# Third layer's experts: tokens sorted by expert into 29 tiles, in place of every expert over every token

## What is computed

```
def _L2_ffn_ref(h, router_w, w1, b1, w2, b2):
    B, S, D, E, F = (2, 256, 128, 14, 256)
    ...
    logits = x @ router_w
    assignments = jnp.argmax(logits, axis=-1)
    probs = jax.nn.softmax(logits, axis=-1)
    weights = jnp.take_along_axis(probs, assignments[:, None], axis=1)[:, 0]
    hid = jnp.einsum('nd,edf->nef', x, w1) + b1
    hid = jax.nn.gelu(hid, approximate=False)
    all_out = jnp.einsum('nef,efd->ned', hid, w2) + b2
    sel = jnp.take_along_axis(all_out, assignments[:, None, None], axis=1)[:, 0, :]
    moe_out = (sel * weights[:, None]).reshape(Bb, Ss, Dd)
...
x = x + jnp.tanh(g_ffn[2]) * _L2_ffn_ref(_layernorm(x, axis=-1), ...)
```

## Time and profile before

| | us |
|---|---|
| median of 3 runs | 1395.78 (1394.82 to 1402.14) |
| the profiled execution | 1410.47 |
| its span | 1408.4 |
| PE busy | 1127.7 (80%) |
| DVE, ACT, POOL busy | 910.1, 788.3, 554.4 |
| granted TensorE clock, mean | 0.882 of full |
| third layer's routing and experts, first and last instruction | 810.94 to 1010.5 |

### The profile page before, as it was taken

The page is one execution under the profiler, slowest core; times in us unless marked ns, Lnnn a source line. Parts: engine busy times, 40 slices in busy tenths (PEclk is TensorE's granted clock), DMA queues, the critical chain, the costliest instruction groups (busy, mean ns, idle before and its releaser), DMA issues. The chain is left out here.

```text
span 1408.4 us, 30563 instructions
## 1 busy us (share of the span) xinstructions
PE 1127.7 (80%) x10377; PEld 540.0 (38%) x10377; DVE 910.1 (65%) x1742; ACT 788.3 (56%) x1471; POOL 554.4 (39%) x611
## 2 busy tenths in 40 slices
PE   3678676887299999998587769999778867786997
PEld 1344453545234444433222343333344533234333
DVE  4668647786666677766689634455568758973454
ACT  2257412674155555554278547888537734883786
POOL 2115102451145555555025227877501201211686
PEclk7779868798599999999779969999979987997899
DMA  6721004110054444442711013323151013100422
GB/s 197 266 93 55 2 0 152 33 34 2 7 139 132 126 125 130 126 132 68 242 32 32 2 40 89 92 90 90 58 176 49 18 62 106 47 3 5 102 90 75
DMA packets 106524, 116.96 MB, mean 83 GB/s; under 512 B 16195, under 2 KB 75787, under 8 KB 105379
## 3 DMA queue, kind: packets, MB, share of 16 engines
q1 hardware_dynamic: 104116, 102.07, 24.7%
q10 hardware_dynamic: 2288, 13.31, 2.6%
HBM read 96.21 MB, written 18.79 MB: 82 GB/s over the span
## 5 line engine op out<-in xcount | busy, mean ns | idle before, releaser
L1295 POOL TENSOR_TENSOR work<-Ks,work 128x512 f16<-128x512 f32 x308 | 356.4, 1157 | 236.9 <-ACT work L1374 228.9
L727 ACT ACTIVATE work<-ps 128x384 f32<-128x384 f32 (+1 forms) x640 | 304.1, 533 | 173.1 <-PE ps L583 106.9
L826 DVE TENSOR_REDUCE bmax<-ps 128x6 f32<-128x768 f32 (+1 forms) x320 | 335.5, 1056 | 69.5 <-PE ps L561 48.4
L1308 PE MATMUL ps<-ao,wf 128*128 128x512 f16 x1320 | 340.5, 384 | 13.8 <-DVEq L1395 6.6
L1418 DVE TENSOR_TENSOR Ks<-ps,Qs 128x512 f32<-128x512 f32 x304 | 210.0, 691 | 151.8 <-ACT ps L1366 123.4
L1324 PE MATMUL ps<-work,wf 128*128 128x512 f16 x924 | 253.8, 384 | 4.7 <-POOL work L1295 3.6
L1308 PEld LDWEIGHTS ps<-ao,wf 128*128 (+1 forms) x1320 | 119.9, 99 | 190.3 <-issue 55.0
L1374 ACT CAST work<-Ks 128x512 f16<-128x512 f32 x308 | 187.7, 610 | 3.8 <-DVE Ks L1418 3.5
L864 POOL TENSOR_SCALAR mx<-bmax 128x16 f16<-128x16 f32 x80 | 24.9, 311 | 377.7 <-DVE bmax L832 218.8
L572 PE MATMUL ps<-Qs,Ks 32*128 32x256 f16 x640 | 124.3, 296 | 56.2 <-issue 19.2
L605 PE MATMUL ps<-work,V 128*9 128x256 f32 (+1 forms) x2560 | 160.3, 371 | 0.0
(11 more groups left out here) (166 smaller groups left out, 1399.6 us busy)
## 6 DMA issues: line engine op xcount, KB each, us to landing
Qs<-scrC SPq DMA_DIRECT2D x256, 128.0 KB, 3.0
Qs<-scrC SPq DMA_DIRECT2D x88, 256.0 KB, 3.1
Qs<-scrQ SPq DMA_DIRECT2D x40, 256.0 KB, 3.1
Ks<-scrK SPq DMA_DIRECT2D x40, 256.0 KB, 3.3
scrK<-work SPq DMA_DIRECT2D x60, 128.0 KB, 2.2
scrQ<-work SPq DMA_DIRECT2D x60, 128.0 KB, 2.6
Qs<-mxT SPq DMA_DIRECT2D x320, 1.0 KB
wf<-in_L_w ACTq DMA_DIRECT2D x2, 1792.0 KB, 9.4
```

Source lines behind the costliest of these rows:

```text
L727: act.activation(prob[:, g % 8, 0:W1], ps[:, 4 + g % 3, 0:W1], ACT.Exp, scale=float(att["dk"]) ** -0.5).then_inc(exped, 1)
L826: dve.tensor_reduce(bmax[:, n // 4 % 2, 2 * (n % 4):2 * (n % 4) + 2, 0:NB], ps[:, b0:b0 + 2, 0:W1].rearrange("p i (n w) -> p i n w", n=NB) ...
L1295: pool.tensor_tensor(hparts[:, (m + r) % 4, 1, :], weighted(m + r), hparts[:, (m + r) % 4, 0, :], ALU.subtract).then_inc(second, 1)
L1308: ins = pe.matmul(out, weight_parts(which, wpart, j), xh[:, xpart, c * CH:(c + 1) * CH], start=(i == 0), stop=(i == 2))
```

## The change

Layer 2 gets a stage of its own, `sorted_stage`, in place of `route_stage` and `expert_stage`.

Routing is as before up to the logits. VectorE then marks each token's first maximum (a matrix M of 0 and 1, with `match_replace`). TensorE counts with M: a product with a strictly triangular matrix gives each token's number among those of its tile with the same expert, and products with ones add the tiles before it. From the totals VectorE works out how many tiles of 128 slots each expert gets, where they start, and so each token's slot (`pos`), and the expert of each of the 29 tiles (`owner`; 16 + 13 tiles hold any distribution). GpSimd writes the 16 tiles of tokens to their slots in DRAM (`scrX`) with indirect DMAs, 128 rows of 512 bytes each. SyncE waits for all of them and loads the slots in eight groups of four tiles (the last of one). TensorE and ScalarE meanwhile load 29 register values each, the offset of every tile's expert.

Then each tile has 6 fp16 matmuls of 128 columns for the first matrix, two activations of 128 columns, a split on VectorE (two instructions of 256 columns), and, two tiles later, 2 matmuls for the bias and 6 for the second matrix, whose result has tokens on partitions. A group's results are copied by ScalarE and written to DRAM (`scrY`) by SyncE. After the last write GpSimd gathers the 16 tiles of tokens back with indirect DMAs, and VectorE adds each, times probability and gate, to `x`, chunk by chunk. Coefficients, their spreading and GpSimd's share of the split are gone.

Outside the stage: the setup makes the triangular matrix, ones, zeros and counters (46 memsets on GpSimd, a transposition, a comparison, a 64 KB load), and layer 0's attention loads 32 KB of `sel` instead of 736 and writes zeros to all of `scrX`, 1.9 MB.

```diff
+TILES = NT + 13
+SLOTS = TILES * P
+GROUPS = (TILES + 3) // 4
...
+            if l == 2:
+                sorted_stage(nc, st, sem, dr)
+                continue
...
+            sp.dma_start(work[:, 4224:4352], dr["causal"][:, 1, :]).then_inc(s_strict, 16)
...
+            for j in range(TILES):
+                pool.memset(st["count"][:, j:j + 1], float(j))
+            pool.drain()
+            for e in range(14):
+                pool.memset(st["tri"][:, e, 0:e + 1], 1.0)
...
-                    for first, last in ((0, SEL_OFF[1]), (SEL_OFF[2], SEL_N)):
-                        sp.dma_start(st["sel"][:, first:last], dr["sel"][:, first:last]).then_inc(st["wsem"][0], 16)
+                    sp.dma_start(st["sel"][:, 0:P], dr["sel"][:, 0:P]).then_inc(st["wsem"][0], 16)
+                    sp.dma_start(st["scrX"].rearrange("(j p) d -> p j d", p=P),
+                                 st["zeros"][:].rearrange("p (o d) -> p o d", o=1).to_broadcast([P, TILES, D])).then_inc(
+                                     st["s_zero"], 16)
...
+            pe.wait_ge(picked, 1)
+            pe.matmul(rank[:, 0:NT, :], st["before"][:], M, start=True, stop=False)
+            pe.matmul(rank[:, NT, :], st["ones16"][:], M[:, 0, :], start=False, stop=False)
+            for t in range(NT):
+                last = NT if t == 0 else NT + 1
+                ins = pe.matmul(rank[:, t + 1:last, :], st["ones16"][:],
+                                bc(M[:, t:t + 1, :], [P, last - t - 1, E]), start=False, stop=(t == NT - 1))
+            ins.then_inc(ranked, 1)
+            pe.wait_ge(numbered, 1)
+            expert = [pe.value_load(at256[:, j:j + 1], min_val=0, max_val=13 * 256) for j in range(TILES)]
...
+            def do_up(j):
+                if j % 4 == 0:
+                    pe.wait_ge(second, j // 4 + 1)
+                if j >= 3:
+                    pe.wait_ge(acted, 2 * (j - 2))
+                for b in range(2):
+                    for i, (wpart, xpart) in enumerate(PRODUCTS):
+                        ins = pe.matmul(ps[:, HB + j % 3, b * P:(b + 1) * P],
+                                        wparts[:, wpart, bass.ds(expert[j] + b * P, P)],
+                                        (xhi, xlo)[xpart][:, j * P:(j + 1) * P], start=(i == 0), stop=(i == 2))
+                ins.then_inc(up, 1)
+
+            def do_down(j):
+                if j == 0:
+                    pe.wait_ge(b2_split, 1)
+                pe.wait_ge(split, j + 1)
+                if j % 4 == 0 and j >= 8:
+                    pe.wait_ge(copied, j // 4 - 1)
+                y = ps[:, YB + j // 4 % 2, j % 4 * P:(j % 4 + 1) * P]
+                for k in range(2):
+                    pe.matmul(y, st["ones16"][0:1, :], b2flat[:, bass.ds(expert[j] + k * D, D)], start=(k == 0),
+                              stop=False)
+                for b in range(2):
+                    for i, (wpart, hpart) in enumerate(PRODUCTS):
+                        ins = pe.matmul(y, hparts[:, j % 3, hpart, b * P:(b + 1) * P],
+                                        wparts[:, wpart, bass.ds(expert[j] + (N * P + b * P), P)], start=False,
+                                        stop=(b == 1 and i == 2))
+                ins.then_inc(down, 1)
+
+            turn_sorted(0)
+            for j in range(TILES + LAGT):
+                if j % 4 == 1 and j // 4 + 1 < GROUPS:
+                    turn_sorted(j // 4 + 1)
+                if j < TILES:
+                    do_up(j)
+                if j >= LAGT:
+                    do_down(j - LAGT)
...
+            bias_at = [act.value_load(at2[:, j:j + 1], min_val=0, max_val=26) for j in range(TILES)]
...
+            first_parts(0)
+            for j in range(TILES):
+                if j % 4 == 1 and j // 4 + 1 < GROUPS:
+                    first_parts(j // 4 + 1)
+                act.wait_ge(up, j + 1)
+                if j >= 3:
+                    act.wait_ge(split, j - 2)
+                for b in range(2):
+                    act.activation(h32[:, j % 3, b * P:(b + 1) * P], ps[:, HB + j % 3, b * P:(b + 1) * P], ACT.Gelu,
+                                   bias=cols[:, bass.ds(bias_at[j] + (C_OFF["b1", 2] + b), 1)]).then_inc(acted, 1)
+                if j % 4 == 3 and j >= 7:
+                    copy_output(j // 4 - 1)
+            copy_output(GROUPS - 2)
+            copy_output(GROUPS - 1)
...
+                dve.match_replace(Dm[:, t, :], only[:, t, :], A[:, t, :], -BIG)
+            dve.drain()
+            dve.tensor_scalar(M, Dm, -BIG / 2, None, ALU.is_le).then_inc(picked, 1)
+            dve.wait_ge(ranked, 1)
+            dve.tensor_scalar(share, rank[:, NT, :], 1.0 / P, None, ALU.mult)
...
+            dve.tensor_copy(pos, posf).then_inc(placed, 1)
...
+                dve.wait_ge(acted, 2 * j + 2)
+                if j >= 3:
+                    dve.wait_ge(down, j - 2)
+                dve.tensor_copy(hparts[:, j % 3, 0, :], h32[:, j % 3, :])
+                dve.drain()
+                dve.tensor_tensor(hparts[:, j % 3, 1, :], h32[:, j % 3, :], hparts[:, j % 3, 0, :],
+                                  ALU.subtract).then_inc(split, 1)
+            for c in range(NC):
+                dve.wait_ge(gathered[c], 64)
+                for t in range(4 * c, 4 * c + 4):
+                    tile = slice(t * D, (t + 1) * D)
+                    dve.scalar_tensor_tensor(x[:, tile], xn[:, tile], coefg[:, t:t + 1], x[:, tile], ALU.mult, ALU.add)
+                added_chunk(nc, st, dve, c, s_var)
+
+        @block.gpsimd
+        def _(pool):
+            pool.sem_clear(ended)
+            pool.wait_ge(b2_in, 16)
+            row = b2row.rearrange("p (e d) -> p e d", e=E)
+            pool.tensor_copy(b2w[:, :, 0, :], row)
+            pool.drain()
+            pool.tensor_tensor(b2w[:, :, 1, :], row, b2w[:, :, 0, :], ALU.subtract).then_inc(b2_split, 1)
+            pool.wait_ge(st["s_zero"], 16)
+            pool.wait_ge(placed, 1)
+            for t in range(NT):
+                pool.indirect_dma_start(scrX, bass.IndirectOffsetOnAxis(ap=pos[:, t:t + 1], axis=0),
+                                        xn[:, t * D:(t + 1) * D], None).then_inc(scattered, 16)
+            for k in range(2):
+                pool.wait_ge(written[k], 16 * ((GROUPS + 1 - k) // 2))
+            for t in range(NT):
+                pool.indirect_dma_start(xn[:, t * D:(t + 1) * D], None, scrY,
+                                        bass.IndirectOffsetOnAxis(ap=pos[:, t:t + 1], axis=0)).then_inc(gathered[t // 4], 16)
+            inverse_deviation(st, pool, s_var)
...
+            sp.wait_ge(scattered, 16 * NT)
+            for gr in range(GROUPS):
+                n = in_group(gr)
+                sp.dma_start(sorted32(gr).rearrange("p (k d) -> p k d", d=D),
+                             scrX[4 * gr * P:(4 * gr + n) * P, :].rearrange("(k p) d -> p k d", p=P)).then_inc(
+                                 sorted_in[gr], 16)
+            for gr in range(GROUPS):
+                n = in_group(gr)
+                sp.wait_ge(copied, gr + 1)
+                sp.dma_start(scrY[4 * gr * P:(4 * gr + n) * P, :].rearrange("(k p) d -> p k d", p=P),
+                             ys[:, gr % 2, 0:n * P].rearrange("p (k d) -> p k d", d=D)).then_inc(written[gr % 2], 16)
```

177 lines of the change are left out of this document (174 added, 3 removed).

## The result

| | before | after |
|---|---|---|
| median of the runs, us | 1397.4 (1394.8 to 1402.1, 4 runs) | 1332.0 (1327.8 to 1332.5, 4 runs) |
| profiled execution: own time, span, us | 1410.5, 1408.4 | 1331.9, 1329.6 |
| third layer's stage in the profile, us | 199.9 | 133.25 |

The changed kernel takes 0.952 of the time of before, 95% interval 0.949 to 0.956: 65 us less, where 47 was forecast. The forecast of 1349 us is 17 us too high; the measured time lies inside its range of 1318 to 1385, and 1 us under the 1333 to 1374 that its own bounds gave.

The account below looks back on a forecast made before the run. The stage was taken as bound by TensorE's columns, 174.9 us of expert matmuls; replacing them with a chain wins 49.3 us, less 2 outside, 47, so median 1395.8 becomes 1349 us, range 1318 to 1385.

Parts of the forecast that it names:

- 3, to the first expert matmul: First tile: four transposes at the low clock 1.2 us, copy and subtraction 0.69 each; first expert matmul at 868.5.
- step 1: Third layer's routing until token places are known: ready at 835.4, nothing won or lost up to there.
- step 5: Copy, write, 16 gathers of 24 us in all, last chunk and tail: stage ends 961.5 against 1010.80.
- Step 4: Loop over 29 tiles at 1.9 us each, 55.1 us, plus 2.7 bare after the last; ends at 926.3.
- rival C: Tile loop slow from fresh weight loads and a low clock: 3.0 us a tile, 32 more, 1381 us; chance 0.13.
- Step 2: 16 scatters at 1.5 us, landing and first group's load: 30.3 us; register loads hidden below 0.88 us each.
- rival D: Indirect DMAs cost what SyncE's do, 0.53 us each: 31 us less, 1318 us; chance 0.10.
- Rival A: GpSimd's indirect DMAs cost 3.5 us each, 64 us more, 1413 us; gain gone from 3.0 each; chance 0.13.
- rival B: Register loads late at 1.9 us each, ending at 895.3 instead of 865.7: 30 us more, 1379 us; chance 0.14.
- Step 6: Outside the stage: setup memsets cost nothing; layer 0's write of zeros delays row maxima, 2 us, from 0 to 8.

Follow-up runs that it names:

- fixed_pe: Changed kernel with TensorE's register loads gone and tile j taking expert j mod 14 at fixed places, ScalarE's registers kept; 1324.9 us, ratio 0.950.
- no_bias: Changed kernel without the two matmuls per tile that add the second bias; 1320.8 us, ratio 0.949.
- gather_twice: Changed kernel with 16 more gathers of the same rows, into a free buffer, before the 16 used; 1347.1 us, ratio 0.968.
- loads_twice: Changed kernel with TensorE loading each of its 29 register values twice; 1341.5 us, ratio 0.962.
- split_late: Changed kernel with GpSimd's split of the second bias starting only after VectorE's last normalised tile; 1319.7 us, ratio 0.945.
- drain_early: Changed kernel with GpSimd draining right behind the issue of its last gather; 1330.4 us, ratio 0.951.
- after_again: The changed kernel run once more without edits; 1326.7 us, ratio 0.950.
- best: Changed kernel with late bias split, early GpSimd drains, early Gelu table, TensorE kept busy during the scatter, one bias matmul a tile; 1314.0 us, ratio 0.942.
- before_again: The kernel before the change, run once more without edits; 1401.8 us.

## Why the prediction was right, and where its sum was off

The mechanism was the forecast one: the 174.9 us of expert matmuls went, and a chain of ranking, scatter, 29 tiles and gathers took their place, with the indirect DMAs below the price at which they would eat the gain. The sum was off by its terms, in before's clock:

| step | predicted | measured | difference |
|---|---|---|---|
| 1, places ready | 835.4 | 828.3 + 10.6 = 838.9 | +3.5 |
| 2, scatter, load, to the first transpose | 30.3 | 25.3 | -5.0 |
| 3, to the first expert matmul | 2.8 | 2.7 | -0.1 |
| 4, loop to the last copy | 57.8 | 44.6 | -13.2 |
| 5, write, to the first gather | 4.0 | 4.3 | +0.3 |
| 5, gathers to the last chunk | 26.6 | 21.3 | -5.3 |
| 5, tail to the next stage | 4.6 | 7.2 | +2.6 |

They add to -17.2, so 66.5 instead of 49.3 us won. Two costs that no term had, 4.6 us for the split in step 1 and 2.6 for the drain in step 5, stand against terms that were put too high. Without them the forecast would have been 24 us too high, so that it came as near as 17 is in part luck.

**Step 4 is the term that was mis-sized.** The pair of load and matmul was put at 0.11 us after three loads in a row. Those stood between 512-column matmuls and had waited for GpSimd, and were no measure of a pace: without register operations a matmul of 128 columns takes 0.071 us (fixed_pe). With them it is 0.090, so a tile of 14 and its transpose take 15 x 0.09 = 1.35 us instead of 1.9, at the full clock. Places from registers do cost something, and more than the 0.2 that was given to them: 0.27. The low clock at the start, rival C's reason, lasted until about 868 (0.60 over 860 to 870) and not through the loop; the 90 matmuls of that window took 10 us instead of 8. Even at the low clock a pair took 0.13 us (39 matmuls in the 5 us from 860, at 0.50) and not rival C's 0.21. That TensorE and not the other engines bounds the loop is shown by no_bias.

**Step 2 and the gathers.** An indirect DMA costs 1.25 to 1.28 us, between the 0.53 of rival D and the 1.5 that was taken; gather_twice shows that its price lies in the issue and that the landing (2.2 us for a scatter, 2.5 for a gather) is paid once. Rival A, from 3.0 us on, did not decide. The 2.0 us that the Trainium skill gives for a DMA from this engine ("DMA: Bandwidth & Descriptors", section "Anatomy of one DMA") are not paid in a row; that most of them is the landing, which the queue hides, is what the rows show. The register loads took 0.65 us each with their operations, under the bound of 0.88, so rival B did not come in; loads_twice shows the threshold where step 2 put it. The floor of about 600 ns that the Trainium skill gives a `tensor_load` ("DMA: Bandwidth & Descriptors", section "Latency and other measured facts") is near that pitch, but the load's own row has 0.30.

**Step 1 left out what the new GpSimd instructions do to VectorE.** The split of the bias stands in no term of the sum, and it held up the normalisation for 4.6 us (split_late): the logits' copy starts at 816.96, 827.6 in before's clock, against 822.98 in the earlier trace rows. The 16 pairs of load and replacement, on the other hand, took 0.15 us each, not 0.208.

**Step 5 left out the drain.** The stage's end was taken over from before, but GpSimd's drain is longer by 0.08 us for each indirect DMA of the stage (drain_early, gather_twice).

**Step 6** was put at 2 us and came out at 0.4. The write of zeros filled the 16 DMA engines, but was done sooner than thought. Windows of the changed kernel in layer 0's attention:

```profile
132.50:139.00 6.50, 5.39 (x138) 2.90 (x126) 5.58 (x10) 5.24 (x13) 3.92 (x6) 1.00 1.00 299
139.00:145.00 6.00, 5.08 (x86) 3.25 (x87) 4.21 (x9) 4.71 (x11) 3.15 (x5) 1.00 0.04 7
```

By 139 it was done (the share of the DMA engines is 1.00 here and 0.04 in the next 6 us), not at 143, and so 2.5 us before the step of the earlier trace rows that needs the maxima. That step now has this row:

```profile
141.46 0.96 DVE L857 TENSOR_REDUCE bmax<-ps 128x6 f32<-128x768 f32 x1 [0.75 <-PE ps L592]
```

VectorE was idle for 0.75 us before it instead of 0.35 (0.76 to 0.78 in after_again, split_late and best, and 0.35 again in before_again). This is read from the trace; doubling the write was not tried.

The setup stage, put at nothing, became shorter: the first normalisation of layer 0 starts at 29.31 and 29.39 us in the two profiles of before, and between 26.2 and 28.5 in the eleven others. The 46 memsets are indeed covered. VectorE waits there for the transfers of the start, which land sooner; why is open. Its rows, of before and then of the changed kernel:

```profile
19.01 0.56 DVE L314 TENSOR_SCALAR work<-work 128x768 f32<-128x768 f32 x1 [6.46 <-DMA work<-in_ident]
```

```profile
16.56 0.56 DVE L343 TENSOR_SCALAR work<-work 128x768 f32<-128x768 f32 x1 [3.95 <-DMA work<-in_ident]
```

**From the stage to the time.** The prediction carried the difference of one stage over to the median. That held: 66.6 to 67.4 us in the stage, 65 and 69 in the medians; the 79 between the first two profiled spans would have misled.

## What to carry to other kernels

A pace taken from an idle corner of a trace is an upper bound, not an estimate: look for a stretch in which the engine issues the same instruction back to back, and where there is none, keep the lower bound in the sum's range with more weight. When work is given to an idle engine, ask which engine it shares something with at that time, and what it leaves behind for the next barrier; both cost here although GpSimd itself was never late. Loads of registers are free up to the moment when the data they wait beside lands, and then cost in full; places that hang on their values are paid for at every matmul in a loop that TensorE's issue bounds. And before a gain of a microsecond or two is put down to an edit, look at the granted clock of the same stretch in both profiles.

## What was not expected of the hardware

- An indirect DMA of 128 rows of 512 bytes costs GpSimd 1.25 us when gathering and 1.28 when scattering; the gathers' pitch was unchanged over 32 in a row.
- GpSimd's drain at the stage's end took 1.10 us without indirect DMAs, 3.73 with 32 and 5.04 with 48: 0.08 us for each.
- Two GpSimd instructions on a single partition (5.3 us) stretched 16 normalisations of VectorE from 4.18 to 8.80 us, and by standing still, not by a slower pace: one of them lasted 3.59 us, the median 0.34.
- A matmul of 128 columns with its own weights takes 71 ns at fixed places and 90 with places from a register, at the full clock; one over a single partition is no cheaper.
- After 25 us of unneeded matmuls TensorE's granted clock was 1.00 for 7 us and then fell to 0.83 in the next 10 us, in which TensorE was busy throughout; in the last kernel, with the same matmuls, it stayed at 1.00. The runs don't say why.
